# In-degree count of a graph network: GpSimd makes one high row in 11 of 19 batches

## The reference

```
deg  = segment_sum(ones(25000), dst, num_segments=50000) + 1
dinv = rsqrt(deg)
msg  = h[src] * (dinv[src] * dinv[dst])[:, None]
agg  = segment_sum(msg, dst) + h * (dinv * dinv)[:, None]
```

## Time and profile before

| what | value |
|---|---|
| time, median of 3 runs | 1655.86 us (1654.5 to 1656.7) |
| the profiled execution's own time | 1654.74 us |
| its span, first to last instruction | 1652.9 us |
| mean granted clock of PE | 0.951 of full speed |
| busy share PE, DVE, ACT, POOL | 88%, 84%, 74%, 60% |
| DMA, whole span | 472.62 MB, mean 286 GB/s |

### The profile page before, as it was taken

How to read it: one execution, slowest core, us unless ns; L and a number is a source line. 1 busy time by engine, 2 the same in 40 slices (tenths; PEclk the granted TensorE clock), 3 DMA queues, 4 the chain that set the end, 5 groups by cost and what they waited for, 6 DMA issues and landing times.

```text
span 1652.9 us, 34140 instructions
## 1 busy us (share of the span) xinstructions
PE 1448.0 (88%) x7522; PEld 1014.6 (61%) x7522; DVE 1385.7 (84%) x4685; ACT 1218.4 (74%) x2989; POOL 992.4 (60%) x1014
## 2 busy tenths in 40 slices
PE   6500999999999977999999998999999999987664
PEld 3200677777777756888887875555555555546553
DVE  7837788888888857888888883999999999988997
ACT  6874355555555535788888885988988889877999
POOL 5000777767767727777777755666676666615442
PEclk9755999999999988999999998999999999998998
DMA  8899899999999856999999888999976666649997
GB/s 308 296 328 370 270 347 350 342 313 282 286 283 284 285 182 214 333 374 370 339 292 304 296 284 254 295 291 295 293 209 181 184 179 178 187 134 336 405 405 278
DMA packets 243446, 472.62 MB, mean 286 GB/s; under 512 B 39192, under 2 KB 40914, under 8 KB 243360
## 3 DMA queue, kind: packets, MB, share of 16 engines
q1 hardware_dynamic: 214672, 412.80, 70.7%
q0 software_dynamic: 28688, 58.89, 15.1%
HBM read 283.30 MB, written 188.24 MB: 285 GB/s over the span
## 4 chain that ended last, share of the span: by engine, by line
PE 75%; DVE 9%; DMA 6%; ACT 4%; POOL 3%; issue 3%; DVEq 0%; SPq 0%; ACTq 0%; POOLq 0%
PE bank L1581 10%; PE bank L1573 10%; PE bank L1612 7%; PE bank L1688 5%; PE bank L1675 5%; PE bank L1563 5%; PE bank L1681 5%; PE bank L1677 5%; PE bank L1680 5%; PE bank L1595 5%; PE bank L1640 4%; DMA XP<-room 4%; DVE gath L1443 3%; POOL gath L833 3%; PE bank L1673 2%
## 5 line engine op out<-in xcount | busy, mean ns | idle before, releaser
L833 POOL DMA_INDIRECT gath<-XP,ROWI x294 | 306.1, 1041 | 179.7 <-issue 67.1
L833 POOL DMA_INDIRECT gath<-MT,ROWI x294 | 305.0, 1037 | 172.3 <-issue 86.2
L833 POOL DMA_INDIRECT gath<-G,ROWI x294 | 280.1, 953 | 115.9 <-issue 86.3
L932 ACT ACTIVATE room<-bank,b_sb 128x512 f32<-128x512 f32 x196 | 123.9, 683 | 156.4 <-PE bank L1573 156.4
L1581 PEld LDWEIGHTS bank<-w_sb,room 128*128 128x128 f32 x1568 | 190.3, 192 | 46.4 <-issue 46.4
L1581 PE MATMUL bank<-w_sb,room 128*128 128x128 f32 x1568 | 190.7, 275 | 0.0
L1573 PE MATMUL bank<-room,w_sb 128*128 128x512 f32 x392 | 184.2, 592 | 0.0
L1612 PE MATMUL bank<-gath,onehot 128*128 128x128 f32 x980 | 139.1, 291 | 21.0 <-DMA gath<-G,ROWI 20.9
L961 ACT ACTIVATE room<-room,st_m,st_r 128x128 f32<-128x128 f32 x384 | 157.1, 481 | 0.0
L940 ACT ACTIVATE room<-bank,DINV 128x128 f32<-128x128 f32 x392 | 111.9, 368 | 58.6 <-PE bank L1581 58.6
L1710 PE MATMUL bank<-ident,room 128*128 128x128 f32 x784 | 109.0, 286 | 47.6 <-ACT room L1061 43.7
(11 more groups left out here) (230 smaller groups left out, 3286.2 us busy)
## 6 DMA issues: line engine op xcount, KB each, us to landing
room<-YT SPq DMA_DIRECT2D x196, 256.0 KB, 4.7
MT<-room SPq DMA_DIRECT2D x98, 260.0 KB, 3.5
XP<-room SPq DMA_DIRECT2D x49, 512.0 KB, 5.1
room<-in_xT SPq DMA_DIRECT2D x98, 256.0 KB
room<-DQ SPq DMA_DIRECT2D x98, 256.0 KB
G<-room SPq DMA_DIRECT2D x98, 256.0 KB
OWN<-room SPq DMA_DIRECT2D x98, 256.0 KB
room<-OWN SPq DMA_DIRECT2D x98, 256.0 KB
```

Source lines behind the costliest of these rows:

```text
L833: nc.gpsimd.indirect_dma_start(gath[k][:, w, 0:width], None, rows, bass.IndirectOffsetOnAxis(ap=ROWI[:, at:at + 1], axis=0)).then_inc(land ...
L932: last = nc.scalar.activation(rows[k], bank[2 + 2 * k + h][:], ACT.Relu, bias=b1_sb[:, h:h + 1])
```

## The change

In the batches of `POOLED`, 11 of the 19, the last of the ten chunks gets its high row from POOL: `pooled_chunk` waits until batch n - 2 is used, and makes (column + hi_s) == 0.5, 392 columns, in a buffer of its own with two slots (`hi_pool`). That is a single 1 and no step, so PE adds it to `bank[0]` and not to `bank[2]`, after a wait on `consts`, which POOL's chunks now raise further. ACT makes three rows and not four in these batches. In POOL's order of work, chunks of batches 2 and 3 stand behind the `c_row` gathers, one chunk (5, 7, 9, 11, 13, 15) ahead of each of the six window gathers, and 16, 17 and 18 behind the last.

```diff
--- before.py
+++ after.py
@@ -39,6 +39,8 @@
 FIRST_COLS = 7 * J
 PAIRS = 5
 STEPPED = 2
+POOLED = [2, 3, 5, 7, 9, 11, 13, 15, 16, 17, 18]
+POOLED_ALONE = 2
 OH_SLOTS = 2
 ET = -(-E // P)
 BATCHES = ET // (2 * PAIRS)
@@ -407,6 +409,7 @@
         oh_lo = early("oh_lo", [P, OH_SLOTS, PAIRS, P, 2], BF16)
         oh_hi = early("oh_hi", [P, OH_SLOTS, PAIRS - STEPPED, NT, 2], BF16)
         step_hi = early("step_hi", [P, OH_SLOTS, 2 * STEPPED, NT + 2], BF16)
+        hi_pool = early("hi_pool", [P, OH_SLOTS, NT], BF16)
         after_lo = oh_lo[:].rearrange("p s n c b -> p (s n c b)").bitcast(F32)
         after_hi = oh_hi[:].rearrange("p s n c b -> p (s n c b)").bitcast(F32)
         win_t, win_u = (after_lo[:, at:at + W * P].rearrange("p (w e) -> p w e", w=W).bitcast(I32) for at in (0, W * P))
@@ -808,16 +811,29 @@
                                     pattern=[[-1, P]], channel_multiplier=1).then_inc(consts, 1)
 
 
+            def pooled_chunk(n):
+                wait(pool, oh_used, n + 1 - OH_SLOTS)
+                at = 2 * (n + 1) * PAIRS - 1
+                nc.gpsimd.tensor_scalar(hi_pool[:, n % OH_SLOTS, :], col_s[:, 1:NT + 1], hi_s[:, at:at + 1], 0.5,
+                                        ALU.add, ALU.is_equal).then_inc(consts, 1)
+
+            pool.wait_ge(oh_ready, 1)
             pool.wait_ge(coarse, 3)
             for w in range(W):
                 nc.gpsimd.indirect_dma_start(c_row[0:NG, w, :], None, dst[0:EP].rearrange("(a b) -> a b", b=ET),
                                              bass.IndirectOffsetOnAxis(ap=coarse_i[0:NG, w:w + 1], axis=0)).then_inc(c_rows, 16)
-            pool.wait_ge(starts_sb, 1)
-            for arr, win in ((src, win_src), (dst, win_dst)):
+            for n in POOLED[:POOLED_ALONE]:
+                pooled_chunk(n)
+            for half, (arr, win) in enumerate(((src, win_src), (dst, win_dst))):
                 flat = arr.rearrange("(a b) -> a b", b=1)
                 for w in range(W):
+                    pooled_chunk(POOLED[POOLED_ALONE + half * W + w])
+                    pool.wait_ge(starts_sb, 1)
                     nc.gpsimd.indirect_dma_start(win[0:NG, w, :], None, flat,
                                                  bass.IndirectOffsetOnAxis(ap=start_i[0:NG, w:w + 1], axis=0)).then_inc(windows, 16)
+
+            for n in POOLED[POOLED_ALONE + 2 * W:]:
+                pooled_chunk(n)
 
             def gathers(n, rows, sums, sums_by_row, width, used_rows, stored):
 
@@ -886,7 +902,7 @@
             for n in range(BATCHES):
                 slot = n % OH_SLOTS
                 wait(act, oh_used, n + 1 - OH_SLOTS)
-                for c in range(2 * STEPPED):
+                for c in range(2 * STEPPED - (n in POOLED)):
                     at = 2 * (n * PAIRS + PAIRS - STEPPED) + c
                     last = nc.scalar.activation(step_hi[:, slot, c, 0:NT + 1], col_s[:], ACT.Sign, bias=hi_s[:, at:at + 1])
                 last.then_inc(steps_ready, 1)
@@ -1516,9 +1532,14 @@
                     pe.wait_ge(steps_ready, n + 1)
                 for b in range(tested, pairs):
                     for c in range(2):
-                        last = nc.tensor.matmul(bank[2][:, 0:NT + 1], oh_lo[:, slot, b, :, c], step_hi[:, slot, 2 * (b - tested) + c, 0:NT + 1],
-                                                start=n == 0 and b == tested and c == 0, stop=n == BATCHES - 1 and b == pairs - 1 and c == 1,
-                                                skip_group_check=True)
+                        if n in POOLED and b == pairs - 1 and c == 1:
+                            pe.wait_ge(consts, CONSTS + POOLED.index(n) + 1)
+                            last = nc.tensor.matmul(bank[0][:, 0:NT], oh_lo[:, slot, b, :, c], hi_pool[:, slot, :],
+                                                    start=False, stop=False, skip_group_check=True)
+                        else:
+                            last = nc.tensor.matmul(bank[2][:, 0:NT + 1], oh_lo[:, slot, b, :, c], step_hi[:, slot, 2 * (b - tested) + c, 0:NT + 1],
+                                                    start=n == 0 and b == tested and c == 0, stop=n == BATCHES - 1 and b == pairs - 1 and c == 0,
+                                                    skip_group_check=True)
                 last.then_inc(oh_used, 1)
 
             pe.wait_ge(w_loaded, 16 * W_LOADS)
```

## The result

| | before | changed |
|---|---|---|
| time, median of 6 runs | 1655.2 us | 1661.35 us (1660.47 to 1664.29) |
| span of the profiled execution | 1652.9 us | 1659.0 us |
| ratio, with its 95% interval | | 1.0037 (1.0026 to 1.0047) |

What follows compares the result with a forecast made beforehand. DVE was taken to pace the in-degree count, with ACT in slack. Eight steady chunks 3.44, plus chunk 5's 0.43, less 0.27, make +3.6 us: 1659.5 us against the median of 1655.86, range 1655.4 to 1662.6.

Steps and rivals of the forecast that it cites:

- What bounds the count: In the in-degree count DVE sets the pace at about 2.05 us a batch; relieving ACT, 5.7 us, wins nothing.
- The stall per chunk: Between oh_lo and oh_hi of a pooled batch, DVE waits 0.43 us (0.35 + 0.08) while POOL reads; chance 0.70.
- the 0.27 that I gave back: In the count's steady part, DVE's waits for PE's release, 12 x (2.0525 - 2.03) us, vanish when pooled batches take longer.
- my lower bound: For DVE's wait at each pooled chunk, the hold alone: 0.32 us, giving +2.6 us in all (1658.5).
- POOL's own time: A POOL row of 392 columns takes 0.62 us, scaled from its TENSOR_SCALAR of the last phase.
- POOL itself has the time: In odd batches a chunk of 0.62 and one gather of up to 1.9 us fit into POOL's 4.1 us.
- Chunks 2 and 3, covered: Their 2 x 0.43 = 0.86 us is hidden in DVE's 2.33 us wait for the c_row gathers.
- Chunk 5: It meets c_rowf and the three c_less, which lead to start_i and batch 4: one stall, 0.43 us.
- The likeliest case: POOL stalls DVE at the boundary between comparisons of the count: 1658.5 to 1661.2 us, +2.6 to +5.3; chance 0.70.
- POOL held off: Rival: in the count POOL gets its turn only when DVE runs dry, 0.76 us a chunk, +6.2 (1662.1); chance 0.11.
- The rival without contention: The count's 16-bit comparisons don't stand in POOL's way, every chunk is hidden: 1655.6 to 1655.9 us; chance 0.13.
- The rival of the clock: Shifting batch 3 by 0.4 us spares PE's clock drop before oh_lo(6), 1.1 us come back: 1658.4; chance 0.06.

Runs made afterwards that it cites:

- e2: The kernel before, with ScalarE making 3 rows and not 4 in the same 11 batches, GpSimd as before; 0.9995 of the time before.
- e4: The changed kernel, with GpSimd making only the first 8 of the 392 columns of each of its rows; 1.0033 of the time before.
- e7: The changed kernel, with GpSimd's operation mult/add and not add/is_equal, and its wait on oh_ready behind the c_row gathers; 1.0017 of the time before.
- e8: The changed kernel with 8 pooled batches and not 11: ScalarE makes all four rows again in batches 16, 17 and 18; 1.0019 of the time before.
- e5: The kernel before, with seven extra GpSimd tensor_scalar operations of different pairs after the DQ stores; one execution, t_b at 58.97 us for 58.28.
- e11: The changed kernel, with GpSimd's chunk a memset of the same 392 columns and its wait on oh_ready behind the c_row gathers; 1.0010 of the time before.
- e10: The kernel before, with 16 matmuls that nothing reads put behind batch 3 on TensorE; 0.9990 of the time before.
- e1: The changed kernel, with GpSimd's wait on oh_ready put behind the three c_row gathers and not ahead of them; 1.0027 of the time before.
- e9: The kernel before, with GpSimd's wait on oh_ready alone added ahead of its wait on coarse and the c_row gathers; 1.0004 of the time before.
- e3: The kernel before, with 14 extra GpSimd tensor_scalar operations of differing types and pairs after the DQ stores; one execution, t_b at 58.45 us.

## Why the prediction held, and where its sum was off

- **What bounds the count** (DVE, with ACT in slack): shown, e2 moved nothing. That a delay goes to the end one for one is borne out by the ratios of eleven kernels, to within some 2 us each and except for e4. That t_b +6.05 became +6.1 in the span is no proof by itself: e2's profiled execution has t_b +0.01 and a span 5.0 longer.
- **The stall per chunk**: 0.43 forecast. Shown is 0.30 to 0.31 in e7, whose eight stretched comparisons add up to 2.45; its B is 2.22 over before, 0.23 less, near the 0.27 that I gave back. In the changed kernel six comparisons are stretched, by 0.31 to 0.36, 2.06 in all. It is near my lower bound (0.32, the hold alone). The handover of 0.1 that I added on top isn't there. The hold doesn't follow POOL's duration: rows of 0.59 and 1.58 us stretch oh_lo by 0.31 and 0.36. The Trainium skill ("SBUF — State Buffer", "Who interferes with whom") calls the ports that the two engines share an exclusive lock. It has the second instruction fully blocked where it speaks of VectorE's two-port modes; of two SBUF inputs it says that they contend with a GpSimd instruction that reads and not with one that only writes. The prediction applied the first to the second. Here DVE stood for 0.36 beside a POOL operation of 1.58, and not at all beside one that only writes, as the section says. The place was off too: in the changed kernel five of six holds fell on an oh_lo, ahead of the batch and not inside it (in e7 three of eight).
- **POOL's own time** is the term that was mis-sized: 0.62 by scaling mult/add, 1.58 measured, since the pair is add/is_equal. With it the step "POOL itself has the time" failed: from 38.03 on POOL goes from chunk to gather to chunk without a pause (2.5 + 1.65 us and two short gaps, 4.45 for two batches), so chunk 16, wanted one batch and not two after chunk 15, comes late, and not "3 us" ahead of PE's need. B of the changed kernel less B of e8 is 2.71. Of this 1.95 are PE's wait at batch 16 (oh_lo(18) begins 4.01 after oh_lo(17), for 2.06), 0.31 the hold of the last oh_hi, and the remaining 0.45 arose in batches 6 to 10, which the three chunks don't touch.
- **Chunks 2 and 3, covered**: only with gathers in time. That the wait on oh_ready stands in front of the gathers, on the path to start_i, I passed over as costing nothing. Through it c_row came 1.47 late, and with the longer spell at the lower clock (DVE's wait before oh_lo(6) 1.52 for 1.08) A came 1.91 late. Of the 1.47, the gathers explain 1.31 (the third ended at 17.20 for 15.89). That the longer spell comes from the change isn't shown: e5 has the same 1.52 with the old count.
- **Chunk 5**: 0.43 forecast, in e7 0.17 (c_rowf took 0.64 for 0.47; oh_lo(4) began at 23.27 for 23.06, 0.04 of it from c_row).

Read from the changed kernel's own timeline: 1.91 (A) + 2.06 (six holds) + 1.95 (PE's wait for chunk 16) + 0.23 (batch 6, 2.44 for 2.21, behind the low clock) = 6.15, against 6.05 of t_b; the last 0.1 is what is left of the 0.27 given back. The forecast of 3.6 had the holds in B too large by 1.4 (3.44 for 2.06), and neither of the other two terms in full (0.43 for A, 0 for POOL). With the slow pair and the wait taken out, e7 gave +2.52.

That the time still fell into the range is in part luck. The likeliest case ended at +5.3; the measured 6.1 lies above it, where only the range's allowance for POOL held off reached (+6.2). The time alone would have spoken for that rival, and the timeline refutes it: in the steady batches DVE never ran dry. The four rows from 38.03 to 51.41 got their turn at the next boundary, others (32.70 here, 39.55 in e7) let one comparison pass. The rival without contention fell with e4 and e11. The rival of the clock was right that the low spell costs this much, but with the change it was longer and not gone; only e10 removed it.

What is open: when POOL gets the next boundary and when it lets one pass, why a wait already reached delays a gather by 0.7 us (by its place, as e1 and e9 show, but not how), why some pairs of operations are slow on POOL, and why the first win_src gather takes 4.6 us in every kernel.

## What to carry to other kernels

Before an engine is relieved, take its work away altogether in an experiment (or check how long its product lies unused): here that would have said "nothing to win" at once. Work given to GpSimd beside VectorE is priced by three things: the exact pair of operations, the columns that it reads while VectorE compares two tensors, and its queue (what the new work holds up, and what stands ahead of it); rows that only write cost nothing here. And a time inside the range, even at a rival's own value, doesn't say which mechanism gave it. An idle TensorE ahead of a dependent chain can be worth some dead matmuls.

## What the runs showed of the hardware

- GpSimd tensor_scalar of 128x392 with a scalar per partition: 0.59 us for mult/add and mult/mult, 1.59 to 1.63 for add/is_equal, add/max, is_equal/mult and add/is_gt, 1.27 for is_equal alone, whatever the types tried (add/is_equal in five pairings of f32, f16 and bf16, mult/add in two, the others from f16 to bf16).
- A GpSimd operation that reads 392 columns stops VectorE's comparison of two SBUF tensors for 0.30 to 0.36 us (e7 and the changed kernel), reading 8 columns for none measurable (e4), and a memset of 392 columns neither stops it nor waits (0.42 us, e11).
- One more reached wait in front of a gather: 0.7 us later (12.89 for 12.18, e9).
- Dead matmuls over 3.7 us of idle time kept the granted clock at 2.4 GHz and brought 1.28 us (e10); without them it fell to 1.2 GHz.
- The same count, executed three times (before, e3, e5), ended at 58.28, 58.45 and 58.97 us, by when a DMA landed and when the clock fell.
